# Decoder layer on one core: the shift of the cross-attention scores by their maxima as a product of an identity with the maxima read at stride zero

## What is computed

```python
q = (queries @ Wq + bq).reshape(N, L, H, D)
k = (keys @ Wk + bk).reshape(N, S, H, D)
v = (values @ Wv + bv).reshape(N, S, H, D)
sm = jnp.einsum('nlhd,nshd->nlhs', q, k) / math.sqrt(D)
sm = jax.nn.softmax(sm, axis=1)
attn = jnp.einsum('nlhs,nshd->nlhd', sm, v).reshape(N, L, H * D)
return attn @ Wo + bo
```

## Time and profile before

| what | value |
|---|---|
| median of 3 runs | 1272.28 us (1270.01 to 1272.82) |
| profiled execution | span 1269.1 us from the first to the last instruction; the profile gives no other time of it |
| PE | 1139.8 us busy (90%), 8658 products |
| DVE | 1067.9 us busy (84%) |
| ACT | 963.9 us busy (76%) |
| POOL | 368.2 us busy (29%) |
| part with the attention's periods | about 90 to 945 us of the span |
| feed-forward block | from about 957 us to the end |

### The profile page before, as it was taken

The page is one execution under the profiler, slowest core; times in us unless marked ns, Lnnn a source line. Parts: engine busy times, 40 slices in busy tenths (PEclk is TensorE's granted clock), DMA queues, the critical chain, the costliest instruction groups (busy, mean ns, idle before and its releaser), DMA issues. The chain is left out here.

```text
span 1269.1 us, 28805 instructions
## 1 busy us (share of the span) xinstructions
PE 1139.8 (90%) x8658; PEld 843.1 (66%) x8658; DVE 1067.9 (84%) x2303; ACT 963.9 (76%) x3173; POOL 368.2 (29%) x445
## 2 busy tenths in 40 slices
PE   1589999999999999999999999999857998878598
PEld 1456666666666667666666666666536977767598
DVE  6259999999999999999999999999863669966698
ACT  1358888888888888888888888888643579768695
POOL 0223334433334333344333344333110013000043
PEclk9989999999999999999999999999977999989799
DMA  5000000001000001000001000010000000000133
GB/s 163 24 16 26 28 22 21 21 21 29 29 19 19 19 19 32 26 19 19 19 23 34 20 19 19 20 37 18 4 8 4 1 1 1 0 1 1 29 105 98
DMA packets 35059, 32.85 MB, mean 26 GB/s; under 512 B 4164, under 2 KB 34748, under 8 KB 35004
## 3 DMA queue, kind: packets, MB, share of 16 engines
q1 hardware_dynamic: 32704, 31.50, 8.3%
q10 hardware_dynamic: 2300, 0.66, 0.3%
HBM read 24.81 MB, written 7.34 MB: 25 GB/s over the span
## 5 line engine op out<-in xcount | busy, mean ns | idle before, releaser
L591 ACT ACTIVATE Px<-score 125x896 f32<-125x896 f32 x128 | 117.4, 917 | 87.7 <-PE score L1119 87.7
L572 ACT ACTIVATE Ps<-score,nmax_s 112x112 f32<-112x112 f32 x512 | 176.2, 426 | 4.0 <-DVE nmax_s L795 4.0
L583 ACT ACTIVATE Px<-score,nmax_h 125x112 f32<-125x112 f32 x512 | 172.6, 367 | 0.6 <-DVE nmax_h L788 0.6
L788 DVE TENSOR_REDUCE nmax_c<-score 125x8 f32<-125x896 f32 x128 | 136.3, 1065 | 13.1 <-PE score L1038 10.3
L572 ACT ACTIVATION_READ_ACCUMULATOR Ps<-score,nmax_s 112x1 f32 x512 | 143.8, 281 | 0.0
L757 DVE TENSOR_REDUCE Zc<-Px 125x8 f32<-125x896 f32 x128 | 138.0, 1078 | 5.3 <-ACT Px L591 1.7
L502 POOL TENSOR_TENSOR Kbd_hi<-Ks_hi,mask 128x448 fp32r<-128x448 f32 x64 | 63.9, 999 | 203.4 <-PE score L1038 137.4
L1130 PE MATMUL outX<-Px,Vn 125*32 125x224 f32 x1536 | 113.2, 367 | 6.9 <-DVE Vn L771 6.9
L583 ACT ACTIVATION_READ_ACCUMULATOR Px<-score,nmax_h 125x1 f32 x512 | 112.9, 221 | 0.0
L1038 PE MATMUL score<-Qbd_hi,KxT_hi 64*125 64x448 f32 x384 | 90.6, 467 | 3.5 <-ACT Px L583 2.4
L1636 PE MATMUL gbank<-xq_hi,w_upT_hi 128*128 128x448 f32 x192 | 73.0, 380 | 22.6 <-DVE up_maxima L1535 12.1
(11 more groups left out here) (246 smaller groups left out, 3566.4 us busy)
## 6 DMA issues: line engine op xcount, KB each, us to landing
ctx_in<-in_ctx SPq DMA_DIRECT2D x32, 375.0 KB
x_in<-in_x SPq DMA_DIRECT2D x32, 112.0 KB, 2.0
x_scratch<-x SPq DMA_DIRECT2D x32, 112.0 KB, 2.0
x2T_all<-x_scratch SPq DMA_DIRECT2D x32, 112.0 KB, 2.1
out<-x2T_all SPq DMA_DIRECT2D x32, 112.0 KB, 1.9
raw_w_up<-in_w_up SPq DMA_DIRECT2D x1, 768.0 KB, 5.6
raw_w_down<-in_w_down SPq DMA_DIRECT2D x1, 768.0 KB, 7.4
raw_w_gate<-in_w_gate SPq DMA_DIRECT2D x1, 768.0 KB, 9.5
```

The lines of the kernel that those rows point to most:

```text
L572: ins = act.activation(Ps[:, g, :], score[slot][0:L, h // QUAD, (h % QUAD) * L:(h % QUAD + 1) * L], ACT.Exp, bias=nmax_s[:, g:g + 1], accu ...
L583: ins = act.activation(Px[u % 2][:, h, :], score[SLOT_OF[f"C{u}"]][0:C, h // QUAD, (h % QUAD) * L:(h % QUAD + 1) * L], ACT.Exp, bias=maxim ...
L591: act.activation(Px[u % 2][:].rearrange("s (q h) l -> s q (h l)", q=2), score[SLOT_OF[f"C{u}"]][0:C, :, 0:QW], ACT.Exp).then_inc(exp_c, 1)
L788: dve.tensor_reduce(dst, score[SLOT_OF[f"C{u}"]][0:C, :, 0:QW].rearrange("s q (h l) -> s q h l", h=QUAD), AX.X, ALU.max, negate=True).then ...
```

## The change

The maxima are written as fp32r numbers, 8 side by side on each of 125 partitions. The shift is made with the weights `unit`, an identity of 125 by 125, and with the maxima themselves as the moving operand, read with a stride of zero over the queries (each maximum 112 times). Since the contraction now runs over 125 partitions, each of the two products takes the whole array in place of a row half. `transpose_max`, `copy_max`, `maxT`, `nmaxT`, `sel`, its two loads and two memsets go. `max_cross` now waits for the product that read its buffer two places before, where it waited for the transpose.

```diff
-        sel = sb("sel", [P, QW], F32R)
+        unit = sb("unit", [C, C], F32R)
...
-        for q in range(2):
-            eng.dma_start(self.sel_raw[HALF_ROWS * q:HALF_ROWS * (q + 1)], self.a["sel"][0:HALF_ROWS, 0:QW])\
-                .then_inc(self.const_ld, 16)
...
-        nmax_c = [sb(f"nmax_c{p}", [C, P]) for p in range(2)]
+        nmax_c = [sb(f"nmax_c{p}", [C, OCT], F32R) for p in range(2)]
...
-                pool.memset(nmax_c[h][:], 0.0).then_inc(consts, 1)
...
-            act.activation(sel[:], sel_raw, ACT.Copy).then_inc(consts, 1)
+            act.activation(unit[:], ident[0:C, 0:C], ACT.Copy).then_inc(consts, 1)
...
-            def copy_max(n, u):
-                i = SHIFTED.index(u)
-                act.wait_ge(nmaxT_done, n.shifts(i + 1))
-                wait(act, shifted, n.shifts(i - 1))
-                act.activation(nmaxT[(n.par * NSH + i) % 2][:, 0:C], maxT[:, 0:C], ACT.Copy).then_inc(nmaxT_copied, 1)
...
-                    wait(dve, nmaxT_done, n.shifts(i - 1))
-                    dst, done = of_halves(nmax_c[(n.par * NSH + i) % 2]), nmax_c_done
+                    wait(dve, shifted, n.shifts(i - 1))
+                    dst, done = nmax_c[(n.par * NSH + i) % 2][:].rearrange("s (q h) -> s q h", q=2), nmax_c_done
...
-            def transpose_max(n, u):
+            def shift(n, u):
+
                 i = SHIFTED.index(u)
                 pe.wait_ge(nmax_c_done, n.shifts(i + 1))
-                wait(pe, nmaxT_copied, n.shifts(i))
-                pe.transpose(maxT[:, 0:C], nmax_c[(n.par * NSH + i) % 2][:], ident[0:C, 0:C]).then_inc(nmaxT_done, 1)
-
-            def shift(n, u):
-
-                i = SHIFTED.index(u)
-                pe.wait_ge(nmaxT_copied, n.shifts(i + 1))
                 for q in range(2):
-                    rows = slice(HALF_ROWS * q, HALF_ROWS * (q + 1))
-                    ins = pe.matmul(score[SLOT_OF[f"C{u}"]][0:C, q, 0:QW], nmaxT[(n.par * NSH + i) % 2][rows, 0:C], sel[rows],
+                    maxima = nmax_c[(n.par * NSH + i) % 2][:, q * QUAD:(q + 1) * QUAD]
+                    ins = pe.matmul(score[SLOT_OF[f"C{u}"]][0:C, q, 0:QW], unit[:],
+                                    maxima.rearrange("s (h o) -> s h o", o=1).broadcast_to([C, QUAD, L]),
                                     start=False, stop=True, skip_group_check=True)
                 ins.then_inc(shifted, 1)
```

More of the change, by code:

```diff
@@ L195, in __init__ @@
         even_odd = sb("even_odd", [P, 2])
-        sel_raw = x2T_all[:, 1, 0:QW]
-        sel = sb("sel", [P, QW], F32R)
+        unit = sb("unit", [C, C], F32R)
         alibi_l = sb("alibi_l", [P, L], BF16)
@@ L201, in __init__ @@
         rows = {"abo": "a_bo", "xbv": "x_bv", "xbo": "x_bo"}
-        N_CONST = len(names) + len(columns) + len(rows) + 8
+        N_CONST = len(names) + len(columns) + len(rows) + 6
         self.w, self.split, self.bcol, self.brow, self.early = w, split, bcol, brow, early
-        self.mask8, self.mask4, self.even_odd, self.sel_raw, self.sel = mask8, mask4, even_odd, sel_raw, sel
+        self.mask8, self.mask4, self.even_odd, self.unit = mask8, mask4, even_odd, unit
         self.alibi_l, self.alibi_r = alibi_l, alibi_r
@@ L348, in attention @@
         w, split, bcol, brow = constants.w, constants.split, constants.bcol, constants.brow
-        mask8, mask4, even_odd, sel_raw, sel = constants.mask8, constants.mask4, constants.even_odd, constants.sel_raw, constants.sel
+        mask8, mask4, even_odd, unit = constants.mask8, constants.mask4, constants.even_odd, constants.unit
         alibi_l, alibi_r, const_ld = constants.alibi_l, constants.alibi_r, constants.const_ld
@@ L380, in attention @@
         x1b = [sb(f"x1b{p}", [L, D]) for p in range(2)]
-        nmax_c = [sb(f"nmax_c{p}", [C, P]) for p in range(2)]
+        nmax_c = [sb(f"nmax_c{p}", [C, OCT], F32R) for p in range(2)]
         nmax_h = [sb(f"nmax_h{p}", [C, OCT]) for p in range(2)]
-        nmaxT = [sb(f"nmaxT{p}", [P, SP // NC + 1], F32R) for p in range(2)]
         Px = [sb(f"Px{p}", [C, OCT, L]) for p in range(2)]
@@ L401, in attention @@
         outX = ctx.enter_context(nc.psum_tensor("outX", [P, KT, 2 * L], F32))
-        maxT = ctx.enter_context(nc.psum_tensor("maxT", [P, BANK], F32))
         consts, mask_done = sem("consts"), sem("mask_done")
@@ L414, in attention @@
         rz_s, rzrep_s, even_s, sum_s = sem("rz_s"), sem("rzrep_s"), sem("even_s"), sem("sum_s")
-        scores_c, nmax_c_done, nmaxT_done = sem("scores_c"), sem("nmax_c_done"), sem("nmaxT_done")
-        nmaxT_copied, shifted, exp_c, nmax_h_done = (sem(n) for n in ("nmaxT_copied", "shifted", "exp_c", "nmax_h_done"))
+        scores_c, nmax_c_done = sem("scores_c"), sem("nmax_c_done")
+        shifted, exp_c, nmax_h_done = (sem(n) for n in ("shifted", "exp_c", "nmax_h_done"))
         z_c, rz_c, vn_done, av_done = sem("z_c"), sem("rz_c"), sem("vn_done"), sem("av_done")
@@ L677, in step @@
                     copy_probs(n4, 0)
-                if n2:
-                    copy_max(n2, 3)
                 if n4:
@@ L699, in step @@
                     hi_keys_cross(n3, 1)
-                if n2:
-                    copy_max(n2, 5)
                 if n4:
@@ L709, in step @@
                     even_self(n4, 0)
-                if n3:
-                    copy_max(n3, 0)
                 if n4:
@@ L727, in step @@
                     exp_self(n5, 0)
-                if n3:
-                    copy_max(n3, 2)
             iterations(act, step)
@@ L739, in _ @@
                 dve.tensor_scalar(bcol[n][:], bcol[n][:], SCALE, None, ALU.mult).then_inc(consts, 1)
-            dve.wait_ge(consts, 13)
+            dve.wait_ge(consts, 11)
             for n in ("xWk", "xWv"):
@@ L773, in normalise_values @@
                     .then_inc(vn_done, 1)
-            def of_halves(t):
-                return t[:].rearrange("s (q x) -> s q x", q=2)[:, :, 0:QUAD]
             def max_cross(n, u):
@@ L1003, in _ @@
         def _(pe):
-            pe.wait_ge(consts, 15)
+            pe.wait_ge(consts, 13)
             pe.wait_ge(bv_spread, 1)
@@ L1196, in step @@
                     values_cross(n4, 0)
-                if n3:
-                    transpose_max(n3, 2)
                 if n4:
@@ L1208, in step @@
                     cross_values(n3, 1)
-                    transpose_max(n3, 3)
                 if n5:
@@ L1236, in step @@
                     transpose_ctx(n5, 0)
-                if n3:
-                    transpose_max(n3, 5)
                 if n4:
@@ L1251, in step @@
                 if n4:
-                    transpose_max(n4, 0)
                     cross_scores(n4, 1)
```

## The result

Median 1284.66 us (1283.37 to 1288.16, 4 runs) against 1271.14 (1268.5 to 1272.82, 4 runs) for the kernel before in the same comparison: a ratio of 1.0112, with a 95% interval of 1.0094 to 1.013. Slower by 13.5 us; forecast was 1286.5, some 14.2 more. Total and growth of the period came as forecast, but several terms behind them did not, and they cancel.

What follows compares the result with a forecast made beforehand. A ring of a PE piece and a DVE piece sets the 27.00 us period; +0.19 and +0.31 make +0.50, over 29.5 periods +14.7, less 0.3 and 0.25: +14.2 on 1272.28, 1286.5 us; range 1277 to 1291.

Steps and rivals of the forecast that it cites:

- The ring: Steady period of 27.00 us as a loop of PE piece and DVE piece; added work in either lengthens it.
- DVE piece: From the end of C4's scores over C3's shift, exponential and sums to `KxT_lo`, about 10 us; predicted +0.31 us.
- with the second product hidden behind the first: Rival: a shift's second product adds no time, the transposes' gain stays; -0.13 us a period, 1268 us; chance 0.07.
- the rival's 0.131: Rival: products in a dense stream come 0.131 us apart; +0.26 us a period, 1279.5 us; chance 0.05.
- PE's wait: No-change rival: PE's 0.36 us of wait at 519.90 takes up the growth; 1271 to 1274 us; chance 0.07.
- the fp32 rate: Rival: stride-zero reads make each shift product take 0.84 us; some 3.8 us a period, about 1390 us; chance 0.04.
- shift of C2, net: In the PE piece, C2's shift was to hold PE 0.21 us longer.
- shift of C0, net: In the PE piece, C0's shift: 0.21 us longer, plus 0.10 for the column groups of `cross_values` behind it.
- transposes in the PE piece: Dropped transposes for C0, C2 and C3 were to give PE back three times 0.11, -0.33 us a period.
- PE piece: From 519.90 to the end of the next batch's C4, about 17 us, PE back to back; predicted +0.19 us.
- The rival that let DVE make up for the later exponential: Only the PE piece grows, as DVE's other waits shrink; +0.19 us a period, 1277.5 us; chance 0.15.
- The terms for the ends: Shorter copy of `sel` at the start, -0.25 us; last period without the detour over transpose and copy, -0.3 us.

Runs made afterwards that it cites:

- one_product runs: Changed kernel without the second shift product of one unit, C0, C2, C3 or C5 in turn: 1283.3, 1282.9, 1281.9 and 1285.5 us.
- one_product_c3: Changed kernel without the second product of C3's shift, so heads 4 to 7 of that unit stay unshifted: 1281.9 us, period 27.32 us.

## Why the prediction was right, and where its steps were off

**The ring held.** Of the signs named in the prediction, the period of 27.5, the exponential 1.06 behind the last scores' start (516.28 to 517.34; forecast 1.01) and the sums right at its end (517.34 + 0.92 = 518.26 to 518.29) came true, and so did PE's wait for `KxT_lo` at 526.90; the two products of a shift, forecast some 0.2 apart, were 0.29 apart. A period grew by 0.50, as forecast, and the one_product runs show that C0 and C2 count through PE and C3 through the DVE piece, while C5 is covered. Rivals: with the second product hidden behind the first the time would have fallen, but it starts 0.29 after it; at the rival's 0.131 the products would have been closer than the 0.19 measured here and the 0.207 of the earlier trace rows; PE's wait took up only its own work between C4 and `KxT_lo`; the fp32 rate would have shown 0.84 where 0.19 stands.

**The terms were off in both directions.** Changes of distances on PE, median over the stretch, against the steps of the prediction:

| term, us a period | forecast | measured |
|---|---|---|
| shift of C2, net | +0.21 | +0.19 |
| shift of C0, net | +0.31 | +0.37 |
| transposes in the PE piece | -0.33 | -0.25 |
| PE piece | +0.19 | +0.31 |
| DVE piece | +0.31 | +0.17 |
| period | +0.50 | +0.50 |

*The shift.* Forecast were 0.30 + 0.207 + 0.207 from the last scores to the next step; measured 0.30 + 0.29 + 0.19 = 0.78. For the first distance I took that of products in a stream, but behind row halves the second load of `unit` is still to come. Part of it returns in the next step: `aWv` holds 0.87 to `transpose_probs` (513.19 to 514.06), where it held 0.96 (506.16 to 507.12), as its first weights are now loaded under the shift. So C2 comes out near the forecast. C0 is followed by groups of columns and gets no such return: 0.87 from the scores to the next step (530.18 to 531.05).

*The transposes.* C3's and C0's gave 0.115 and 0.106, but C2's 0.03: the values product behind it held 0.20 to the next one (504.27 to 504.47) and holds 0.20 without the transpose too (511.03 to 511.23 in the profile after), so that only the transpose's own start of 0.03 went. I had read the 0.20 as part of its cost.

*The DVE piece.* C3's sums came 0.37 later (1.60 for 1.23), not 0.31, for the same 0.29. But from there to the end of `KxT_lo` it is now 526.84 - 518.29 = 8.55, where it was 519.85 - 511.10 = 8.75. In the kernel before, DVE waited once more in this stretch, by the list of waits of 200 to 852 us:

```profile
DVE Qs_lo L804 <- ACT Qs_hi L604: 2.6, 17, 0.2
```

That row (0.15 each time) is missing after the change. The prediction said that DVE "has no wait left between 511.10 and 519.85 that is long enough"; it had one that gave half of the delay back. Behind it stands a path that the prediction left out, over ACT's list. PE, ACT and DVE before, then ACT and DVE after:

```profile
509.96 1.15 PE L1067 MATMUL work<-xT,aWk 128*128 128x112 f32 x8
511.14 0.60 ACT L604 ACTIVATE Ks_hi<-work,abk 128x112 fp32r<-128x112 f32 x2
514.53 0.63 ACT L604 ACTIVATE Qs_hi<-work,abq 128x112 fp32r<-128x112 f32 x2
515.19 0.58 DVE L804 SCALAR_TENSOR_TENSOR Qs_lo<-work,abq,Qs_hi 128x112 fp32r<-128x112 f32 x2
```

```profile
521.52 0.64 ACT L591 ACTIVATE Qs_hi<-work,abq 128x112 fp32r<-128x112 f32 x2
522.19 0.57 DVE L780 SCALAR_TENSOR_TENSOR Qs_lo<-work,abq,Qs_hi 128x112 fp32r<-128x112 f32 x2
```

In both kernels `Qs_lo` starts 0.03 after the end of `Qs_hi` (515.16 to 515.19, 522.16 to 522.19; 0.032 to 0.035 in every period of the loop), so that ACT releases DVE there in both, now with a wait too short for the list. From `Ks_hi` to `Qs_hi` ACT works without idle time (3.39 and 3.37 us). Before, `Ks_hi` started 0.03 after the keys products `work<-xT,aWk` that PE makes behind C3's shift (end 511.11), and 0.99 after the start of C3's exponential; now it starts 0.81 after that start (517.34 to 518.15), right behind the exponential. So the exponential had 0.18 of room. From C4's scores `Ks_hi` comes 0.18 later (511.14 - 509.45 = 1.69, 518.15 - 516.28 = 1.87), and about that is what the DVE piece grew by. In one_product_c3 the exponential and the keys products both come 0.18 earlier, so that run cannot tell the two apart. The step that was wrong is thus "sums and all behind them with it": in the loop the sums did not set when `KxT_lo` ends. The rival that let DVE make up for the later exponential was right for a part. So 0.19 + 0.31 was forecast, and 0.31 + 0.17 came, with 0.02 that these rows don't place: two errors of 0.12 and 0.14 that cancel. That the period came out at 0.50 to the second digit was luck.

**Outside the steady periods.** The first 28 periods together, from the first `work<-xWo` to the one at which the last three begin, took 758.5 and 758.7 us in the two profiles of the kernel before and 773.7 in that after: +15.1, near the +14.7 of 29.5 periods. But six of the 28, those written out ahead of and behind the loop, went from 27.36 to 28.05, +0.69 each. DVE in one of them, before and after:

```profile
834.21 1.09 DVE L788 TENSOR_REDUCE nmax_h<-score 125x8 f32<-125x896 f32 x1 [0.82 <-PE score L1038]
835.36 1.09 DVE L757 TENSOR_REDUCE Zc<-Px 125x8 f32<-125x896 f32 x1
839.95 0.56 DVE L804 SCALAR_TENSOR_TENSOR Qs_lo<-work,abq,Qs_hi 128x112 fp32r<-128x112 f32 x2
```

```profile
847.27 1.09 DVE L764 TENSOR_REDUCE nmax_h<-score 125x8 f32<-125x896 f32 x1 [0.70 <-PE score L1014]
848.79 1.09 DVE L736 TENSOR_REDUCE Zc<-Px 125x8 f32<-125x896 f32 x1 [0.42 <-ACT Px L584]
853.38 0.56 DVE L780 SCALAR_TENSOR_TENSOR Qs_lo<-work,abq,Qs_hi 128x112 fp32r<-128x112 f32 x2
```

Here the path of the prediction holds: the sums start 1.52 after the maxima, where it was 1.15, and from them to `Qs_lo` it is 4.59 in both kernels, so that nothing of the 0.37 is given back (in the loop 4.09 became 3.90). With the 0.31 of the PE piece that makes 0.68. The terms for the ends (-0.25 and -0.3) cannot be told: the first `work<-xWo` started at 123.14 and 122.11 in the two profiles before, 122.28 after, and the last three periods took 70.1, 72.7 and 70.8. The copies, costed at nothing, cost nothing: ACT waits for L1089 by more than it did for L1119 (114.0 us against 66.1 in the stretch).

**A term that I did not have.** The feed-forward part is 3 us shorter, with the same code. Most of it is in the 288 gate products, 0.207 apart in both profiles before and 0.200 after:

```profile
1013.70 0.36 PE L1602 MATMUL gbank<-xq_lo,w_gateT_hi 128*128 128x448 f32 x1
1013.90 0.36 PE L1603 MATMUL gbank<-xq_hi,w_gateT_lo 128*128 128x448 f32 x1
```

288 times 0.007 is 2.0; that all of it reaches the time is argued, not shown. In the experiments it is 0.200 too, except in one_product_c3, where the median is 0.206, though its code differs from that of the other three one_product kernels in one number only. What decides between the two stays open. Without these 3 us the change would have cost some 16, and the forecast of 14.2 would have been low.

## What to carry to other kernels

Two products that run side by side in halves of the array are one product's time; an edit that makes each of them use all rows at least doubles that time (here 0.20 to 0.48), and whatever it saves elsewhere has to be larger than this first. Cost a product behind a change of the array's tiling by its whole path (its entry, the weight loads that could not run ahead, what the next step gets back), not by the distance in a steady stream. Before you add a delay along a chain, see at every step which of the instructions it waits for came last, short waits included: a second path that is nearly as late takes part of the delay away. A step that looks free to move may hold a buffer or stand ahead of a copy that another engine needs: before moving it, read who waits for its consumer, and what is queued behind that.

## What was not expected of the hardware

- After products in row halves, PEld stood idle until the whole-array product itself started: the first two weight loads of 125 x 125 ended 0.29 us later, and only then did the second product begin. The third load ran ahead under a product again. The Trainium skill, page "TensorEngine Tiling (Array Packing)", section "Key Properties", says that a change of the tiling mode drains TensorE. The trace agrees, and gives the price: 0.30 in place of 0.20 into the whole array, and 0.29 in place of 0.19 to the second product there, 0.09 of which the next step got back.
- A moving operand of 4 numbers a row, each read 112 times at stride zero, runs at the full rate: 0.19 us for 448 columns, no slower than the 0.200 to 0.207 of a plain operand. The Trainium skill, page "SBUF — State Buffer", section "Door 1: The DMA port swizzle", says that consecutive accesses to the same 16-byte line run at full bandwidth; for a moving operand of PE the trace agrees, with these 0.19 us.
- The same gate products came 0.200 or 0.207 us apart in different kernels; the granted clock was 1.00 in both (stretches of 25 us around the rows, with 122 products before and 127 after).
